# Attention over 16 positions inside the cross-attention's loop, last block

## The reference

```python
x = x + _L3_xattn_ref(ctx_1024, _layernorm(x), ...)   # 16 heads of 64, 257 keys + 32 latents per batch
x = x + _L3_attn_ref(_layernorm(x), w_qkvw, w_out)    # this layer is moved
x = x + _L3_ffn_ref(_layernorm(x), ...)               # 16 heads, then 8 experts, top 2

# _L3_attn_ref, H = 16, G = 4, HD = 2; x is 64 x 32 x 128
qkvw = x @ w_qkvw                      # 512 columns, 4 chunks c of (q, k, v, w) x 32
q, k, v = (t.reshape(B * G, H, -1, HD).swapaxes(1, 2) for t in (q, k, v))
attn = softmax(q @ k.swapaxes(-2, -1) * HD ** -0.5)
o = (attn @ v).swapaxes(1, 2).reshape(B, S, dim)
return o * w.reshape(B, S, dim) @ w_out
```

## Time and profile before

| | |
|---|---|
| time, 3 runs | 2199.0 us (2197.55 to 2201.45) |
| profiled execution | 2197.9 us, span 2196.0 us |
| busy over the span | PE 83%, DVE 69%, ACT 45%, POOL 33% |
| mean granted TensorE clock | 0.913 of 2.4 GHz |

### The profile page before, as it was taken

One profiled execution on the slowest core, in us unless ns is written; L12 is line 12 of the kernel. 1 busy time (PEld: TensorE's weight loads), 2 busy tenths in 40 slices (PEclk: granted clock), 3 DMA queues, 4 the chain that ended last, 5 costly groups with the idle time before them and its releaser, 6 DMA issues. The chain is left out here.

```text
span 2196.0 us, 50176 instructions
## 1 busy us (share of the span) xinstructions
PE 1829.5 (83%) x20226; PEld 1199.1 (55%) x20226; DVE 1516.6 (69%) x3637; ACT 981.1 (45%) x2482; POOL 730.3 (33%) x951
## 2 busy tenths in 40 slices
PE   6678999899888799985778699999999987656496
PEld 4324557555655556542657556666666652234386
DVE  6799995688866755557851676766666569987732
ACT  5536654566634712242313355555555421115243
POOL 2244554455531524204340501000000046533543
PEclk9779999999989999997879899999999998867688
DMA  8000000100036000160044101000000000021087
GB/s 339 1 1 0 1 0 1 73 5 4 5 146 243 4 1 1 77 251 1 2 142 136 31 20 39 20 11 20 20 10 10 1 1 10 19 98 71 31 289 240
DMA packets 57670, 130.63 MB, mean 59 GB/s; under 512 B 13961, under 2 KB 36188, under 8 KB 51808
## 3 DMA queue, kind: packets, MB, share of 16 engines
q1 hardware_dynamic: 54144, 121.32, 15.4%
q0 software_dynamic: 3296, 6.12, 0.9%
HBM read 107.97 MB, written 20.12 MB: 58 GB/s over the span
## 5 line engine op out<-in xcount | busy, mean ns | idle before, releaser
L319 POOL TENSOR_TENSOR arena<-arena 128x4 f32<-128x4 f32 (+2 forms) x97 | 113.9, 1176 | 804.2 <-DVE arena L263 347.1
L3290 ACT ACTIVATE arena<-PS,arena 128x289 f32<-128x289 f32 x256 | 127.0, 506 | 178.2 <-DVE arena L3395 178.2
L1870 POOL TENSOR_TENSOR arena<-arena 128x128 f32<-128x128 f32 x384 | 140.8, 407 | 42.9 <-PE PS L1733 19.1
L3178 PE MATMUL PS<-arena 128*128 128x289 f32 x512 | 135.5, 408 | 2.3 <-DVE arena L3389 1.8
L1806 DVE RECIPROCAL arena<-PS 128x128 f32<-128x128 f32 x96 | 91.5, 954 | 52.6 <-PE PS L1771 52.5
L1837 ACT COPY arena<-PS 32x128 f32<-32x128 f32 x384 | 99.5, 259 | 47.4 <-PE PS L1747 42.5
L1256 POOL TENSOR_TENSOR arena<-arena 128x512 f32<-128x512 f32 x64 | 84.0, 1313 | 109.8 <-DVE arena L1401 109.8
L366 PE MATMUL PS<-arena 128*128 128x512 f32 x176 | 96.9, 686 | 12.6 <-DVEq L4201 11.8
L3178 PEld LDWEIGHTS PS<-arena 128*128 128x128 f32 x512 | 92.2, 190 | 24.2 <-issue 2.6
L3395 DVE TENSOR_REDUCE arena<-PS 128x2 f32<-128x578 f32 x128 | 92.5, 753 | 7.3 <-PE PS L3178 6.1
L458 PE MATMUL PS<-arena 128*128 128x128 f32 (+4 forms) x576 | 83.3, 291 | 10.9 <-DVE arena L413 4.1
(11 more groups left out here) (420 smaller groups left out, 4780.7 us busy)
## 6 DMA issues: line engine op xcount, KB each, us to landing
arena<-in_ctx SPq DMA_DIRECT2D x32, 1091.0 KB, 11.1
arena<-in_f_w SPq DMA_DIRECT2D x39, 514.0 KB, 5.3
arena<-in_ctx SPq DMA_DIRECT2D x16, 834.0 KB, 16.5
lists<-arena SPq DMA_DIRECT2D x8, 1040.0 KB, 10.8
arena<-in_f_w SPq DMA_DIRECT2D x32, 256.0 KB, 3.0
arena<-in_ctx SPq DMA_DIRECT2D x16, 512.0 KB, 3.8
arena<-in_mid SPq DMA_DIRECT2D x1, 3796.5 KB, 11.9
arena<-in_late SPq DMA_DIRECT2D x1, 3204.0 KB, 10.2
```

Of the source, the lines that this page charges most:

```text
L319: e.tensor_tensor(x, x, half.broadcast_to(list(x.shape)), ALU.pow).then_inc(*T.done("norm_root", tag))
L1870: k = e.tensor_tensor(dst[:, b], spread(src[:, b, :], [P, HG, S], 1), spread(self.g.C["headmask"], [P, HG, S], 2), ALU.mult)
L3178: m = e.matmul(PS[:, k, 0:UL], self.qt[i % 2][:, j, P * k:P * k + P], self.kt[i % 3][:, j, :], start=True, stop=True)
L3290: e.activation(self.weights(n, k, 0, UL), PS[:, k, 0:UL], ACT.Exp, bias=self.st[:, h, k:k + 1], accum_out=self.st[:, h, 4 + k:5 + k]).then ...
```

## The change

Layer 10 is worked by quarters of the batches (q: tiles 4q to 4q + 3, 16 batches) and no longer by chunks. A partition is now a chunk, a half of the heads and one of 16 batches. Quarters 0 to 2 are worked inside L3Cross's loop; quarter 3, the rest of quarter 2, and the transfers and projections of all come behind the loop.

For quarters 0 to 2 there are four units of 4 x 256 scores each (12 units in all). A unit has six passes of 128 x 1024 on GpSimd (`PASSES_AT`), three reductions of VectorE (`maxima`, `total`, `mix`) and one exponential of ScalarE; none of it is in PSUM. The tables give the step, n = 25 + 16 q + d. For q = 2, d goes to 9 in the loop; what is left stands in `rest`. For quarter 3 the old way is kept, with two units of 8 x 256 scores over 128 partitions, and the GpSimd passes left over stand in front of and between its products.

```diff
 # L3Cross
     def answer(self, n):
-        return ("k3_oT_dve" if n % 2 else "k3_oT_act"), n
+        return "k3_oT_act", n                      # likewise query(): ScalarE from tile 1 on
 # sp: behind the loads of tiles 13 and 14, and behind the last
+            if i == 13: self.inner.store(e, T, 0)
+            if i == 14: self.inner.fetch(e, T, 0)
+        self.inner.store(e, T, 1); self.inner.fetch(e, T, 1)
 # act, step n: both answers, queries 1 and 3, key_scale in j == 2 (before: 1)
+            self.inner.norm_act(e, T, n)
+            self.inner.step_act(e, T, n)           # at the end of the step
 # pool: follows the steps n
-        for i in range(2, NT): ...
+        for n in range(NB + BT - 1):
+            self.inner.step_pool(e, T, n)
+            (roots of the latents at j == 0, keys(i + 2) and extra(i + 2) at j == 1)
 # dve, step n: no odd answers, no queries from tile 1 on
+                self.key_var(e, T, i + 2)          # j == 1 (before: in key_stats, j == 0)
+                self.key_norm                      # j == 2 (before: 1)
+                self.key_gain                      # j == 3 (before: 2), key_shift stays at 3
+            self.inner.step_dve(e, T, n)           # at the end of the step, behind the add to x
 # pe
+            self.inner.step_pe(e, T, free, n)
 # L3Attn
+    PASSES_AT = {0: (("first", 0), ("second", 0)), 1: (("sums", 0), ("first", 1)), 2: (("second", 1), ("sums", 1)),
+                 3: (("less", 0), ("first", 2)), 4: (("second", 2), ("sums", 2)), 5: (("less", 1), ("weigh", 0)),
+                 6: (("weigh_more", 0), ("less", 2)), 7: (("weigh", 1),), 8: (("weigh_more", 1),), 9: (("first", 3), ("second", 3)),
+                 10: (("sums", 3), ("weigh", 2)), 11: (("weigh_more", 2),), 12: (("less", 3),), 14: (("weigh", 3),),
+                 15: (("weigh_more", 3),)}
+    START = 25
+    MAXIMA_AT, TOTAL_AT, MIX_AT = {2: 0, 3: 1, 5: 2, 11: 3}, {5: 0, 7: 1, 10: 2, 14: 3}, {8: 0, 9: 1, 12: 2, 16: 3}
+    EXP_AT = {4: 0, 6: 1, 7: 2, 13: 3}
+    Z_AT = {22: ((0, 7),), 23: ((1, 5), (2, 4)), 24: ((3, 7),)}
+    def features_pe(self, e, T, free, q, k, b):    # 4 blocks k of a quarter, at n = 16 q + Z_AT
+        for j in range(4):
+            h = 4 * k + j
+            for c in range(4):
+                m = e.matmul(g.PS[S * c:S * c + S, b, P * j:P * j + P], self.xT[q % 2][:, S * h:S * h + S], w_[:, P * c:P * c + P], ...)
+    def store(self, e, T, q, half=None):           # waits for m3_mixed
+        for c in range(4):
+            for r in range(2):                     # 16 partitions each
+                e.dma_start(t["mixed"][c][...][:, :, lo:hi], self.o[at:at + BG, :, lo:hi])
+    def fetch(self, e, T, q, half=None):           # waits for the stores, then 4 loads
+    def pass_pool(self, e, T, what, U):            # each one tensor_tensor of 128 x 1024
+        first: a = q0 * k0    second: b = q1 * k1    sums: a = a + b    less: a = a - maxima
+        weigh: b = a * v1     weigh_more: a = a * v0
+    def maxima_dve: tensor_reduce(least, a, max)   # 128 x 64 <- 128 x 1024; waits for sums
+    def total_dve:  tensor_reduce(total, a, add)   # waits for the exponential
+    def mix_dve:    reciprocal(total); tensor_reduce(mixed, ab, add)  # 128 x 128 <- 128 x 2048; waits for weigh_more
+                    mixed *= total; two products with the gate
+    def exp_act:    activation(a, a, Exp)          # waits for less
+    def stats_dve, root_pool, apply_act, turn_pe, turned_act: norm and turning of one tile, each a few small instructions
 # L3Attn behind the loop
+    def pool(self, e, T):
+        self.root_pool(e, T, NT - 1)
+        for what, U in rest[:-2]: self.pass_pool(e, T, what, U)    # sums 3, weigh 2, weigh_more 2, less 3
+        products(0)
+        for what, U in rest[-2:]: self.pass_pool(e, T, what, U)    # weigh 3, weigh_more 3
+        products(1); weighed(0); weighed(1); norm roots of the next layer
+    def dve(self, e, T):
+        self.stats_dve(NT - 1); total(2); maxima(3); features_out(1); features_out(3)
+        products(0); residual(0), residual(1); products(1); mix(2); maxima "end 0"; total(3); maxima "end 1"; mix(3)
+        weigh(0); weigh(1); mix "end 0"; mix "end 1"
+        for q in range(2, NQ):
+            residual(q, q - 2); self.after.begin_rows_dve(e, T, q - 2)
+        self.after.begin_rows_dve(e, T, NQ - 2)
+    def pe: turn_back(0), (1); turn tile 15; 4 blocks of quarter 3; output(0), (1);
+            add_products(0); subtract(0); add_products(1); subtract(1); turn_back and output of 2 and 3
+    def sp: store(2); fetch(2); store(3, half 0); store(3, half 1); fetch(3)
 # L3Ffn: a "quarter" of the norm is now every fourth tile (q::NQ), so the turning of each waits for all four
-        cols_pe(e, T, g, "f3_h", self.hr, free, range(4), warm=(2, 0, 0, 1))
+        cols_pe(e, T, g, "f3_h", self.hr, free, range(4), lambda q: [("normed", ("f3_h", x)) for x in range(NQ)], warm=(2, 0, 0, 0))
```

More of the change, by code:

```diff
@@ new lines, in stats_at, with blocks_at, unit_at, passes_at @@
+    def stats_at(self, n):
+        t, j = divmod(n - 7, 4)
+        return t if j == 0 and 0 <= t < NT else None
+    def blocks_at(self, n):
+        for q in range(self.LAST):
+            for k, b in self.Z_AT.get(n - 16 * q, ()):
+                yield q, k, b
+    def unit_at(self, n, table):
+        for q in range(self.LAST):
+            u = table.get(n - 16 * q - self.START)
+            if u is not None:
+                yield self.NU * q + u
+    def passes_at(self, n):
+        for q in range(self.LAST):
+            for what, u in self.PASSES_AT.get(n - 16 * q - self.START, ()):
+                yield what, self.NU * q + u
@@ new lines, in fetch @@
+    def fetch(self, e, T, q, half=None):
+        for w in T.due((f"m3_back{q}", (half, "out", 3, 1))):
+            e.wait_ge(*w)
+        for c in range(4):
+            e.dma_start(self.back[q][:, c, :], self.g.t["mixed"][c][self.BG * q:self.BG * q + self.BG].rearrange(
+                "b (i d) -> (b i) d", d=D)).then_inc(*T.done(f"m3_back{q}", c, 16))
+    def sp(self, e, T):
+        self.store(e, T, 2)
+        self.fetch(e, T, 2)
+        for half in range(self.NE):
+            self.store(e, T, self.LAST, half)
+        self.fetch(e, T, self.LAST, self.NE - 1)
@@ L3530, in subtract @@
             w_ = 2 * NP
[L3531 to L3533 removed]
+            for n, b in enumerate(range(4 * u, 4 * u + 4)):
+                x = spread(self.least_end[:, u, w_ * n:w_ * n + w_], [P, w_, NP], 2)
+                for w in T.due(("m3_least", ("end", u))):
                     e.wait_ge(*w)
@@ new lines, in pe, with norm_act @@
+        self.turn_pe(e, T, free, NT - 1, 2)
+        for k in range(4):
+            self.features_pe(e, T, free, self.LAST, k, 4 + k)
+            free[4 + k] = ("m3_z_dve" if k % 2 else "m3_z_act"), (self.LAST, k)
+        for q in range(2):
+            output(q, q)
+        add_products(0)
+        subtract(0)
+        add_products(1)
+        subtract(1)
+        for q in range(2, NQ):
+            turn_back(q, q - 2)
+            output(q, q - 2)
+    def norm_act(self, e, T, n):
+        t = self.normed_at(n)
+        if t is not None:
+            self.apply_act(e, T, t)
@@ new lines, in root_pool, with step_pool @@
+    def root_pool(self, e, T, t):
+        g = self.g
+        root_pool(e, T, g, g.small[:, t, 7:8], ("m3", t), ("norm_var", ("m3", t)))
+        for w in T.due(("norm_root", ("m3", t))):
+            e.wait_ge(*w)
+        e.tensor_tensor(g.small[:, t, 1:2], g.small[:, t, 0:1], g.small[:, t, 7:8], ALU.mult).then_inc(*T.done("norm_shift", ("m3", t)))
+    def step_pool(self, e, T, n):
+        for what, U in self.passes_at(n):
+            self.pass_pool(e, T, what, U)
+        t = self.stats_at(n)
+        if t is not None:
+            self.root_pool(e, T, t)
@@ new lines, in pool, with stats_dve @@
+        weighed(0)
+        weighed(1)
+        for q in range(self.LAST):
+            self.after.begin_pool(e, T, q)
+    def stats_dve(self, e, T, t):
+        s = self.g.small[:, t, :]
+        for w in T.due(("k3_added", t)):
+            e.wait_ge(*w)
+        e.bn_stats(s[:, 0:6], self.g.X[:, t, :]).then_inc(*T.step())
+        for w in T.due(T.prev()):
+            e.wait_ge(*w)
+        e.bn_aggr(s[:, 6:8], s[:, 0:6]).then_inc(*T.step())
+        for w in T.due(T.prev()):
+            e.wait_ge(*w)
+        e.tensor_scalar(s[:, 0:1], s[:, 6:7], -1.0, None, ALU.mult).then_inc(*T.step())
+        e.tensor_scalar(s[:, 7:8], s[:, 7:8], 1e-5, None, ALU.add).then_inc(*T.done("norm_var", ("m3", t)))
@@ L3656, in dve @@
+        self.stats_dve(e, T, NT - 1)
+        mixes, totals, maximas = ([self.unit(u) for u in self.rest(x)] for x in (self.MIX_AT, self.TOTAL_AT, self.MAXIMA_AT))
+        self.total_dve(e, T, totals[0])
+        self.maxima_dve(e, T, maximas[0])
+        features_out(1)
+        features_out(3)
         products(0)
+        for q in range(2):
+            residual(q, q)
```

(31 more changed lines are left out.)

500 lines of the change are left out of this document (330 added, 170 removed).

## The result

The changed kernel takes 2207.4 us (median of 9 runs, 2203.7 to 2209.0), the kernel before 2197.8 on the same chip: ratio 1.004, 95% interval 1.0029 to 1.0052. It is slower by 0.4%, where 2154 was forecast. The profiled execution has a span of 2206.1 us against 2196.0.

What follows compares the result with a forecast made beforehand. TensorE was taken to bound the loop, DVE the attention behind it. 2197.9 - 196.6 + 102 + 4 + 17 + 27 + 1.5 = 2152.8, with the median's 1.1 about 2154 us; range 2112 to 2194.

Steps and rivals of the forecast that it cites:

- DVE, ScalarE and GpSimd in the loop: In the loop, GpSimd's passes and DVE's longer list delay products before TensorE's turning: 0.65 us in 42 steps, +27 (-12 to 109).
- the moves: In the loop, odd answers' and queries' copies go from DVE to ScalarE; TensorE's 12.5 us wait might vanish, low end -12.
- features and turns: On TensorE in the loop: 12 feature blocks at 1.3 us, 15 turns of a tile at 0.1 each; +17 (11 to 45).
- Rival 2: Before every turning, at L3408: TensorE waits a whole GpSimd pass, 2.6 us in 42 steps, 109 instead of 27; 2236, chance 0.12.
- Rival 1: In the loop: DVE's freed waits hide all but TensorE's part, 27 becomes 0 or down to -12; 2127, chance 0.27.
- Rival 3: TensorE's feature blocks in the loop run one behind another, 44 us instead of 16; 2182, chance 0.05.
- Rival 4: GpSimd falls behind its table, passes pile up behind the loop or VectorE waits in mid-list, 26 us; 2180, chance 0.09.
- The stage behind the loop: The attention left behind the loop, from its fence's opening, takes 102 us (88 to 120) in place of the old 196.6.
- Last add to the fence: At the loop's end, a mix and GpSimd's weigh_more hold up all four engines' fence: +4 (0 to 12).
- The exchange: Behind the loop, stores and loads between the last gate and the turning: 11 us, where 6.0 were taken before.
- gate product: Behind the loop, DVE's last sums, division and gate end 78.8 us after the stage opens.
- The begin of the next layer: After the stage, every quarter's turning waits for all four and twelve transposes no longer overlap the last norm: +1.5.

Runs made afterwards that it cites:

- run 7: Changed kernel with GpSimd's passes cut to 64 elements and VectorE's maxima, totals and mixes to two rows, moved quarters' attention not computed: 0.949 of the kernel before.
- run 4: Kernel before with only copies of odd answers and queries moved to ScalarE and key work a step later, no attention in the loop: 0.989.
- run 3: Changed kernel with one more GpSimd wait: a step's passes start only after VectorE's four products before the turning; 0.978 of the kernel before.
- run 8: run 3 plus new orders: third-step mix before the add of X, and GpSimd and VectorE work reordered behind the loop; 0.968 of the kernel before.
- run 5: run 4's kernel plus 66 GpSimd passes on a spare buffer nobody waits for, released by VectorE's maxima; 1.000 of the kernel before.
- run 9: run 4's kernel plus the same 66 idle GpSimd passes as run 5, released later, by ScalarE's second exponential; 1.001 of the kernel before.
- run 10: Changed kernel with products in the form that also writes a sum, plus run 8's new orders, without the added wait; 0.974 of the kernel before.
- run 11: run 8 plus another pass table: at most one pass in steps with the keys' gain and shift, waiting for the shift; 0.963 of the kernel before.
- run 13: run 11 plus another order behind the loop: GpSimd's last-quarter first product before a subtracting pass, VectorE's second product behind two residuals; 0.959 of the kernel before.
- thin passes: Changed kernel with GpSimd's passes of the moved quarters cut to 64 elements, all waits kept, their attention not computed; 0.962 of the kernel before.

## Why the prediction was wrong

**The step that failed** is the term for "DVE, ScalarE and GpSimd in the loop", 0.65 us in each of 42 steps, +27. Against the kernel before, the loop grew by 102.3 us where 17 + 27 = 44 were forecast. By experiment: the moves -19.2; features and turns +21.2 (run 7 less run 4), near the 17; VectorE's list and GpSimd's passes 17.5 + 82.8 = +100.3. So the failed term is -19.2 + 100.3 = +81, three times its size, and the 54 missing us are the miss: 2154 + 54 = 2208.

*Why it was too small.* It priced a meeting at half a pass, once per pair of products, times the share of time in which a pass is in flight, as the earlier trace rows has it: 0.5 for each of 84 pairs, 42 us, of which it let 27 through. There one GpSimd instruction met one of VectorE's. In the loop 34 products were stopped, about as many as that share gives of 84 pairs; but each lost 2.1 us. In the trace 30 of the 34 had over 80% of a pass still ahead of them: VectorE and GpSimd started nearly together, or GpSimd had its next pass ready when the first product ended, and the second product waited for that one too. That makes 70 us. The pattern stood in the earlier trace rows: two and two took 12.11 and 16.82 us, in turns. The prediction used that row for the stage behind the loop, but took the friendlier row for the loop.

*What else it left out.* It priced only the products' meetings. The mix's three small products (0.29 and 0.23 us alone, 7.2 in a bad place) met passes as well, 14 us in all, and the key statistics 3. The keys' gain and shift did not:

```profile
L3169 DVE TENSOR_TENSOR arena<-arena 128x1024 f32<-128x1024 f32 x14 | 17.1, 1225 | 0.5
L3163 DVE TENSOR_TENSOR arena<-arena 128x1024 f32<-128x1024 f32 x14 | 17.0, 1212 | 0.0
```

The kernel before has 1215 ns for both; they met passes only in runs 3 and 8, where the wait puts the passes beside them, and in 5 and 9. And with TensorE's waits its granted clock fell: the 256 matmuls of L3236 and L3237 took 151.8 us, 20.8 more than before; for the clock compare the 0.90 above with the earlier trace rows. That was in the text as a thing to watch and had no price.

*The slack.* "The list's slack hides part": right in kind, shown by runs 5 and 9, where 66 passes, of 1.9 to 2.0 us, cost 24 to 27 us of the loop beside a short list. But here it hid almost nothing: VectorE's instructions took 87 us longer and the loop 83, for the new VectorE work, which the sum put at +73 us, stands in the same list.

**Rival 2** (GpSimd's passes stop VectorE in front of every turning, 109 instead of 27, 2236) had the mechanism and the place. Its point of decision, 1.7 us lost per step, was passed: 81 / 42 = 1.9 us, or 100.3 / 42 = 2.4 without the moves' gain. Its time is 29 us too high, mainly since the moves' gain of 19 was left out of it. Its picture, one whole pass in every step, is not what the trace shows: 23 steps had a stopped product, some of them several. The Trainium skill's page SBUF — State Buffer gave its rule in the section "SBUF: two separate sides"; the weight of 0.12 was far too low for a rule that two groups of rows bore out. Its argument "passes cover only a third of the loop" counts time, but the two engines mostly start together, as at 1528.48 and 1528.51. And its other argument, that VectorE kept its turn in the attention's pair row, misreads the row: the prediction's own sum for it, 4.88 + 3.6 + 3.6, has a whole GpSimd instruction between VectorE's two. **Rival 1** (the loop hides all) is out. **Rival 3**: the last quarter's 128 matmuls took 5.04 us, four blocks, 1.26 each, so the forecast's 1.3 holds. **Rival 4**: VectorE never waited in mid-list for GpSimd in the loop; out.

**What held.** The stage behind the loop: 104.9 us, forecast 102. Last add to the fence: 4.1, forecast 4. The exchange: 10.0 us from VectorE's last gate product (to 1951.17) to the turning (1961.18), forecast 11. That gate product was forecast 78.8 us behind the opening and ended at 83.2. Two idles had not been seen:

```profile
1904.44 2.85 POOL L3801 TENSOR_TENSOR arena<-arena 128x1024 f32<-128x1024 f32 x1 [13.37 <-DVE arena L3869]
1921.06 2.29 DVE L3921 TENSOR_REDUCE arena<-PS 128x128 f32<-128x2048 f32 x1 [16.71 <-PE PS L3673]
```

GpSimd waited for a total that stood behind maxima on VectorE, so its second product ended 44 us into the stage and not 35, and TensorE's adding and VectorE's maxima came after it; runs 8, 10, 11 and 13 with the other order need 98.4 to 99.0 us. **The moves** had been priced only as the end of a range, -12; they give -19 of the loop. The begin of the next layer had +1.5; from the fence on the profiles differ by -2.6, but such differences between executions are larger than the term. The range's low edge, 2112, is 3 below the sum given for it, 2154 - 27 - 12 = 2115, which changes nothing here.

## What to carry to other kernels

Before work goes to an idle GpSimd beside a busy VectorE, list VectorE's instructions with two SBUF inputs or from SBUF to SBUF ahead of what the critical engine waits for, and price each at a whole GpSimd instruction where the two can start together, not at half of one: a train of passes and a train of short products alternate. Then place the passes, with a wait if need be, behind those instructions; the same work went from 0.4% slower to 4.1% faster by waits and order alone. And a change made of a move and a new load is judged by its parts: the moves alone were worth 1.1%, which the load hid.

## What the runs showed of the hardware that was not expected

- VectorE's products from SBUF to SBUF and GpSimd's passes alternated one for one where both had work ready (2 products in 5.23 us beside passes of 2.54 and 2.60, 0.65 alone). With the sum written out, the same products (0.51 and 0.08 us) pass beside GpSimd without a wait, 73 of 73.
- How long a stopped instruction is does not matter: one over four elements took 164 ns in the median and 2571 beside a pass.
- A short wait of TensorE can cost more than itself: behind 3.02 us of it in run 8 the granted clock was 0.53 from 1622.7 to 1626.3, 1.00 before, and two matmuls that take 1.02 us took 1.87, about one of TensorE's two levels of 1.2 and 2.4 GHz against the other. In the kernel after the granted clock of the loop's later part was 0.90, with thin passes 0.99.
- GpSimd's instructions with two inputs over 1024 elements took 1.9 to 2.9 us by their operands: 1.9 for a product of one buffer with itself, 2.0 for subtracting the maxima, 2.35 for adding two buffers, 2.6 and 2.9 for the products with q and k and with v. That it is the broadcast that costs is not shown, since the subtraction has a broadcast operand too.
